# Graph attention kernel: softmax weights regrouped into four chunks of 128 rows and one of 32-row bands, row sums moved to VectorE, block-diagonal values written by DMA

## The reference

```python
def _gat_attention(self_feat, cond_adj, label_bias, Wq, bq, Wk, bk, Wout, bout):
    kv = self_feat[:, :20]                      # B, 20, 512
    qh = (self_feat @ Wq.T + bq).reshape(B, N, 16, 32)
    kh = (kv @ Wk.T + bk).reshape(B, 20, 16, 32)
    aff = einsum('bnhd,bmhd->bnhm', qh, kh) / sqrt(32)
    aff = where(cond_adj[:, :, None, :] > 0, aff, -9e15) + label_bias[:, :, None, :]
    w = softmax(aff, axis=-1)
    out_t = einsum('bnhm,bmf->bnhf', w, kv)
    return (einsum('bnhf,hgf->bnhg', out_t, Wout) + bout.reshape(16, 32)).reshape(B, N, 512)

row_zero = v.sum(-1) == 0
vcq = concat([v, where(row_zero[..., None], 0.0, q[:, None, :])], -1)
self_feat = vcq @ W_self.T + b_self
output = self_feat
for d in range(2):                              # d = 0: adj, d = 1: its transpose, first 20 targets
    output = output + _gat_attention(self_feat, A[d].sum(-1), A[d] @ w_bias + b_bias, Wq[d], ...)
return v + relu(output)
```

## Time and profile before

| | |
|---|---|
| runs | 735.38, 736.54, 736.55 us; median 736.54 |
| profiled execution | span 733.6 us from the first to the last instruction; its own time is not listed apart from the three |
| instructions | 11543 |
| busy | PE 676.3, DVE 625.7, POOL 519.8, ACT 413.0 us |
| mean granted clock of TensorE | 0.984 of full speed |
| moved by DMA | 70.64 MB, 96 GB/s on average |
| first scores / last batch's scores begin | 85.5 / 696.0 us |

### The profile page before, as it was taken

The page is one execution under the profiler, slowest core; times in us unless marked ns, Lnnn a source line. Parts: engine busy times, 40 slices in busy tenths (PEclk is TensorE's granted clock), DMA queues, the critical chain, the costliest instruction groups (busy, mean ns, idle before and its releaser), DMA issues.

```text
span 733.6 us, 11543 instructions
## 1 busy us (share of the span) xinstructions
PE 676.3 (92%) x3824; PEld 600.2 (82%) x3824; DVE 625.7 (85%) x802; ACT 413.0 (56%) x718; POOL 519.8 (71%) x436
## 2 busy tenths in 40 slices
PE   6999899998989989998989989998999989998975
PEld 6867788898878978798888978798788978798774
DVE  4656699989998889989998899889898899889863
ACT  3536355665656464764656464764566464765523
POOL 0000398949796688949796798949796798949795
PEclk9999999999999999999999999999999999999996
DMA  9634505124241505124241506033241406032101
GB/s 339 276 119 92 159 19 137 56 77 105 75 116 30 156 31 140 50 78 108 71 115 46 151 19 172 18 99 101 77 112 60 123 18 172 18 105 86 38 31 57
DMA packets 54080, 70.64 MB, mean 96 GB/s; under 512 B 25136, under 2 KB 34608, under 8 KB 53424
## 3 DMA queue, kind: packets, MB, share of 16 engines
q1 hardware_dynamic: 54064, 70.44, 32.6%
HBM read 49.68 MB, written 20.75 MB: 96 GB/s over the span
## 4 chain that ended last, share of the span: by engine, by line
PE 54%; DVE 25%; issue 10%; POOL 5%; DMA 3%; ACT 2%; POOLq 0%; SPq 0%; DVEq 0%; ACTq 0%
PE gen L369 10%; PE gen L371 10%; PE gen L370 10%; PE aff L405 7%; PE aff L424 7%; DVE xs L657 5%; DVE xl L652 4%; PE tp L434 4%; DVE xs L659 3%; PE gen L376 3%; DVE sfl L663 3%; POOL sff L922 3%; DVE z L704 2%; DVE sff L679 2%; POOL z L873 2%
## 5 line engine op out<-in xcount | busy, mean ns | idle before, releaser
L873 POOL TENSOR_TENSOR z<-cb,bx 128x320 f32<-128x320 f32 x128 | 127.0, 1013 | 46.9 <-PE tp L371 46.9
L424 PE MATMUL aff<-gh,sfh 128*128 128x320 f32 x512 | 126.1, 328 | 9.4 <-DVE sfl L663 7.0
L424 PE MATMUL aff<-gl,sfh 128*128 128x320 f32 x512 | 117.7, 311 | 0.0
L424 PE MATMUL aff<-gh,sfl 128*128 128x320 f32 x512 | 117.3, 311 | 0.0
L922 POOL TENSOR_TENSOR sff<-sff,x 128x512 f32<-128x512 f32 x64 | 83.3, 1312 | 40.8 <-ACT sff L535 40.6
L424 PEld LDWEIGHTS aff<-gh,sfh 128*128 128x128 f32 x512 | 87.6, 191 | 22.1 <-DVE sfl L663 10.4
L887 POOL TENSOR_TENSOR z<-z,mx 128x640 f32<-128x640 f32 x64 | 93.4, 1459 | 15.2 <-DVE mx L706 13.4
L369 PE MATMUL gen<-xh,w1h 128*128 128x512 f32 x256 | 101.6, 397 | 0.0
L371 PE MATMUL gen<-xh,w1l 128*128 128x512 f32 x256 | 99.9, 390 | 0.0
L370 PE MATMUL gen<-xl,w1h 128*128 128x512 f32 x256 | 99.8, 390 | 0.0
L891 POOL TENSOR_TENSOR z<-z,rcp 128x640 f32<-128x640 f32 x64 | 81.7, 1276 | 19.8 <-DVE rcp L712 19.8
(11 more groups left out here) (89 smaller groups left out, 1497.3 us busy)
## 6 DMA issues: line engine op xcount, KB each, us to landing
x<-in_x SPq DMA_DIRECT2D x64, 256.0 KB, 4.5
out_y<-sff SPq DMA_DIRECT2D x64, 256.0 KB, 2.7
msk<-in_mask SPq DMA_DIRECT2D x16, 880.0 KB, 4.8
cb<-c_scratch SPq DMA_DIRECT2D x16, 320.0 KB, 3.3
v_scratch<-x SPq DMA_DIRECT2D x16, 160.0 KB
vc<-v_scratch SPq DMA_DIRECT2D x16, 160.0 KB, 4.7
wkT<-in_wkT SPq DMA_DIRECT2D x1, 2048.0 KB, 9.8
woT<-in_woT SPq DMA_DIRECT2D x1, 2048.0 KB, 16.0
```

What stands on the lines that cost most here:

```text
L424: mm = nc.tensor.matmul(aff[:, t % 2, half, 0:SH], s, g[:, f, slot, half * SH:(half + 1) * SH], start=(f == 0 and i == 0), stop=(f == FC - ...
L873: last = nc.gpsimd.tensor_tensor(z[:, t, :].rearrange("p (g d h m) -> p g d h m", g=HG, d=D, h=H4)[:, :, d], cb[:].rearrange("p (g d h m) ...
```

## The change

The order of the 640 columns becomes (head group, head, direction, key). Of the 20 keys the first 16 of each (head, direction) make four chunks of exactly 128 rows, one for each head group; the last 4 make a fifth chunk `zr`, with 32 rows for each head group. `attend` is one group of three matmuls for each head group; `attend_rest` adds 12 matmuls over 32 rows each. Their output goes to the banks `aff` and not to `gen`, so that the next scores wait for the additions that read it.

The values are stored in two scratch tensors, and `load_v` writes them straight into the diagonal blocks of `va` and `vr`, which POOL clears once: 20 transfers where there was one, behind the outputs of the batch. POOL's `v_blocks` goes; its normalise is split in two (4 of 20 keys, then 16).

The row sums come from a second copy of x with nodes on partitions (`xn`), loaded in two halves, one batch further ahead (b + 2). DVE reduces them, a flag for each node goes to DRAM and comes back to all partitions (`store_nonzero`, `load_nonzero`). PE's `row_sums` and DVE's `x_sums` go.

b_self is left out of the self feature and added to the query bias (`query_bias`, in the prologue) and the output bias, so `sf_high` has one activation. The key products are made in eight units between the halves of `self_feat`. DVE takes 2 chunks of `xl` and 1 of `sfl` (before 3 and 2), POOL the rest. On ACT the first labels move ahead of `x_high`. In the prologue wq and xn are loaded ahead of woT.

```diff
-            def load_v(b):
-                sp.dma_start(vc[:].rearrange("p c t g -> p c (t g)"),
-                             v_dram[bass.ds(b, 1)].rearrange("o (c p) e -> p (o c) e", p=P)).then_inc(s_vin, 16)
+            def load_v(b):
+                own = va_dram[bass.ds(b, 1)].rearrange("o (h d) m (k e) -> h (o d m) k e", h=H4, e=DH)
+                rest = vr_dram[bass.ds(b, 1)].rearrange("o (h d) m (g t e) -> h g (o d m) t e", h=H4, g=HG, t=2)
+                for h in range(H4):
+                    r = h * D * MA
+                    sp.dma_start(va[r:r + D * MA, :, :, h].rearrange("p g t e -> p (g t) e").bitcast(F32), own[h]).then_inc(s_vin, 16)
+                for j in range(HG):
+                    for h in range(H4):
+                        r = (j * H4 + h) * D * MR
+                        sp.dma_start(vr[r:r + D * MR, :, h].bitcast(F32), rest[h, j]).then_inc(s_vin, 16)
...
             def batch(b, slot, i, ahead):
                 if ahead == 2 and slot == 0:
                     sp.wait_ge(s_bd, i + 1)
                     load_k(i + 1)
+                if ahead == 2:
+                    for half in range(2):
+                        sp.wait_ge(s_rsum, b * 2 + 4 + half)
+                        load_rows(b + 2, half)
                 if ahead >= 1:
                     sp.wait_ge(s_bx, b * T + T)
                     load_c(b + 1)
-                if ahead >= 2:
+                if ahead == 2:
+                    store_nonzero(b + 2)
                     sp.wait_ge(s_mk, b + 2)
                     load_mask(b + 2)
-                if ahead >= 1:
-                    sp.wait_ge(s_vb, b + 1)
-                    load_v(b + 1)
+                    sp.wait_ge(s_sfq, b * FC + 2 * FC)
+                    load_nonzero(b + 2)
                 for j in range(HG):
                     sp.wait_ge(s_y, b * HG + (j + 1))
                     sp.dma_start(out[bass.ds(b, 1), :, j].rearrange("o p n -> p (o n)"), sff[slot][:, j, :]).then_inc(s_out[slot], 16)
...
+                if ahead >= 1:
+                    sp.wait_ge(s_pv, b * HG + HG)
+                    load_v(b + 1)
```

```diff
 PE
+                if u < 2 and not first:
+                    pe.wait_ge(s_z, pair * (2 * T) - 1 + u)
+                if u >= 2:
+                    pe.wait_ge(s_gl, pair * GU + (u - 1))
...
+                    if t < 2:
+                        pe.wait_ge(s_u, b * HG + (2 * t + 2))
-                        if ahead >= 1 and t == T - 1 and f == FC // 2:
-                            row_sums(b + 1, 1 - slot)
...
+            def attend_rest(b, slot, pair):
+                pe.wait_ge(s_vin, b * (16 * VD) + 16 * VD)
+                pe.wait_ge(s_wtl, chunk(b, 1))
+                pe.wait_ge(s_z, b * T + T)
+                if slot == 1 and pair is not None:
+                    pe.wait_ge(s_gl, pair * GU + GU)
+                for k, (t, w) in enumerate(((0, wth), (0, wtl), (1, wth))):
+                    for j in range(HG):
+                        r = slice(j * H4 * D * MR, (j + 1) * H4 * D * MR)
+                        nc.tensor.matmul(pv_bank(j), vr[r, t].rearrange("p h e -> p (h e)"), w[r, 0, :], start=(k == 0), stop=False)
 DVE
-            def x_sums(n, slot):
-                dve.wait_ge(s_xh, n * FC + FC)
-                nc.vector.tensor_tensor(xs[:], x[slot][:, 0:2], x[slot][:, 2:4], ALU.add).then_inc(s_xs, 1)
-                dve.wait_ge(s_xs, n * 2 + 1)
-                nc.vector.tensor_tensor(xs[:, 0], xs[:, 0], xs[:, 1], ALU.add).then_inc(s_xs, 1)
+            def row_sums(n, half, src, s_in, count):
+                dve.wait_ge(s_in, count)
+                nc.vector.tensor_reduce(rsum[:, 2 * half:2 * half + 2], src, AX_X, ALU.add).then_inc(s_rsum, 1)
...
                 total(b, 0)
+                if ahead == 2:
+                    row_sums(b + 2, 0, xn[:], s_xnin, b * 32 + 48)
                 shift(b, 2)
-                if ahead >= 1:
-                    nonzero(n, other)
                 total(b, 1)
+                if ahead == 2:
+                    row_sums(b + 2, 1, xn[:], s_xnin, b * 32 + 64)
+                    nonzero(b + 2, True)
                 shift(b, 3)
```

More of the change, by code:

```diff
@@ L371, in parts, with self_feat @@
                 return nc.tensor.matmul(acc, ll, rh, start=False, stop=last)
-            def row_sums(n, odd):
-                pe.wait_ge(s_xs, n * 2 + 2)
-                nc.tensor.matmul(gen[:, bank(RS[odd]), :], ones[:], xs[:, 0, :], start=True, stop=True).then_inc(s_rs, 1)
-            def self_feat(n, odd, f):
+            def self_feat(n, f, between=None):
                 if f >= 2:
                     pe.wait_ge(s_sfq, n * FC + (f - 1))
-                if f == 1:
-                    pe.wait_ge(s_nz, n + 1)
-                acc = gen[:, bank(SF[odd] + f), :]
                 cols = slice(f * P, (f + 1) * P)
@@ L411, in scores, with key_products @@
-            def scores(b, slot, pair, ahead):
+                    mm = parts(gen[:, f % 2, :], (w1h[:, c, cols], w1l[:, c, cols]), (xh[:, c, :], xl[:, c, :]), c == 0, c == FC - 1)
+                    if between is not None and c % 2 == 1:
+                        if c == FC - 1:
+                            mm.then_inc(s_sf, 1)
+                        key_products(between, 2 * f + c // 2)
+                if between is None:
+                    mm.then_inc(s_sf, 1)
+            def key_products(pair, u, first=False):
+                f, k = u // G2, u % G2
+                if u == 0:
+                    pe.wait_ge(s_bd, pair + 1)
+                if u < 2 and not first:
+                    pe.wait_ge(s_z, pair * (2 * T) - 1 + u)
+                if u >= 2:
+                    pe.wait_ge(s_gl, pair * GU + (u - 1))
+                for hg in (2 * k, 2 * k + 1):
+                    for d in range(D):
+                        mm = nc.tensor.matmul(aff[:, k, hg % 2, 0:SH].rearrange("p (b h d m) -> p b h d m", b=2, h=H4, d=D)[:, :, :, d],
+                                              wq[:, hg, d, f * P:(f + 1) * P], bd[:, hg * D + d], start=True, stop=True)
+                mm.then_inc(s_g, 1)
@@ L480, in batch @@
                 if ahead >= 1:
-                    self_feat(n, odd, FC - 1)
-                if next_g:
-                    key_products(i + 1, 1)
+                    self_feat(n, FC - 1, pair)
                 transposes(b, slot, 2)
+                attend_rest(b, slot, pair)
                 transposes(b, slot, 3)
-                for j in range(HG):
-                    attend(b, slot, j, ahead)
-                    if next_g and j < 2:
-                        key_products(i + 1, j + 2)
-                    if j + 4 < SC:
-                        transposes(b, slot, j + 4)
+                attend(b, 0)
+                transposes(b, slot, 4)
+                for j in range(1, HG):
+                    attend(b, j)
             batches(pe, batch)
@@ L562, in _ @@
                                      bias=bself[:, c:c + 1]).then_inc(s_sfkh, 1)
-            for c in range(FC):
-                x_high(0, 0, 0, c)
             act.wait_ge(s_wo, 16)
@@ L799, in batch @@
                 shift(b, 0)
+                shift(b, 1)
                 if ahead >= 1:
@@ L900, in _ @@
             bias(0, 1)
-            sf_low(0, 0)
+            for f in range(FC - FL):
+                sf_low(0, 0, f)
             def batch(b, slot, i, ahead):
@@ L914, in batch @@
                 sub_max(b, 3)
-                normalise(b, 2)
-                normalise(b, 3)
-                v_blocks(b)
+                for t in range(2, T):
+                    normalise_rest(b, t)
+                    normalise(b, t)
                 if ahead >= 1:
-                    sf_low(n, 1 - slot)
+                    for f in range(FC - FL):
+                        sf_low(n, 1 - slot, f)
                 for j in range(HG):
```

542 lines of the change are left out of this document (292 added, 250 removed).

## The result

| | before | after |
|---|---|---|
| time, median | 735.99 us (735.38 to 736.55, 4 runs) | 901.16 us (899.86 to 904.66, 4 runs) |
| ratio | | 1.2249, 95% interval 1.2222 to 1.2276 |
| profiled execution, span | 733.6 us | 902.9 us (its own time 904.66) |
| mean granted clock | 0.984 | 0.893 |

A forecast was written before the change was run, and what follows sets the result against it. PE was taken as the bound (92% busy), DVE right behind. Loop start 87.5, fourteen batches 732, the last two 69.5 and 2.9 outside the span gave 892, rounded to 890 us; range 815 to 945.

The forecast's parts named there:

- The stall: 20 value-load issues on SP, 10.8 us, delay the row load; DVE's reduction waits 10 us, holding up the softmax and PE.
- T: Time in us since the scores of a batch started on PE.
- The period: Loop batches with the delayed rows: 48.7 us even and 56.9 odd, 105.6 a pair against 81.7 before.
- The other terms: Outside the seven pairs: loop start at 87.5 us, batch 0 7.5 us sooner, batches 14 and 15 34.5 and 35.
- The bands: PE's 12 attend matmuls of 32 rows each: taken at 0.9 us together, between 0.7 and 2.8.
- The clock: PE idles over 8 us in each batch and drops to its lower clock: 1.5 us a batch added.
- the rival on the other side: SP's 20 value loads issue in about 1 us, rows land when DVE asks: 723 us, 705 to 735; chance 11%.
- R + 33.3: Odd batch's length, counted from R, when the first row load lands: 55.4 us before the clock's addition.
- POOL about even, and no faster: POOL loses value blocks, gains an xl, an sfl and a split normalise: about even, no faster at the softmax's end.
- R + 24.6: Even batch's length, counted from R, when the first row load lands: 47.2 us before the clock's addition.

The follow-up runs named there:

- the experiment with one quarter: The changed kernel with all 12 band matmuls reading rows 0 to 31, instead of four quarters of the rows: 939.8 us (1.276).
- either mend: The changed kernel with the value loads moved behind the row loads on SP's queue (788.2 us), or with DVE's two row reductions moved later (789.2 us).
- four moved groups of lines: Kernel with two row buffers and the first g evicted earlier (779.4 us), plus reorderings on POOL, on DVE and ACT, and in the prologue: 739.2 us (1.004).

## Why the prediction was right, and where it was not

- **The stall.** SP's timeline, point by point: x at T = 6.7 (said 6.6), the 20 issues 10.3 us from the first to the last's end, 11.0 to the next issue (10.8), the row load at T = 18.85 (18.4), DVE's reduction at T = 23.3 (22.6). The two kinds of load are not equal, 0.76 and 0.46 apart, and only their mean fits the 0.54 I took: that the size came out so well is in part luck. The Trainium skill (DMA: Bandwidth & Descriptors, Anatomy of one DMA) gives its dispatch of some 50 ns in the account of a transfer issued from GpSimd, as one part of its fixed cost. It was no price for an issue on SP's queue, and the 0.46 and 0.76 us measured here are what such an issue takes of it.
- **The period.** Even batches of the loop behind the first took 49.2 to 49.9 us (48.7), odd ones 55.8 to 57.4 (56.9). Total 0 ended at T = 13.6, not 12, so DVE waited 9.7 and not 10; nothing hung on it.
- **The other terms.** The loop starts at 90.7, not 87.5: the key-bias products behind the last key start at 45.89 where they started at 39.65, 6.2 us later, not 3.4, and ACT waits 8.4 us for the stores of values, which I had not looked at. The 14 batches took 736.7 (732), since batch 0 gained less from its early value loads, 45.8 us (41.2). Batches 14 and 15 took 37.0 and 38.5 (34.5 and 35). Together 3.2 + 4.7 + 6.0 = 13.9, the whole difference between 889 and the span of 902.9.
- **The bands** took 0.90 us, exactly as taken. No row of before could tell 0.7 from 2.8; the reason given for the lower end, a quarter of the rows for each, is what the experiment with one quarter bears out.
- **The clock.** The lower level after the stall, as said (0.50); 1.5 us a batch taken, 0.7 to 1.1 an even batch gained when it was kept up.
- **What failed: the rival on the other side.** It said that with cheap issues the kernel would be faster, 723 us, with the sign turning near 0.1 us an issue. The runs show no such point, though none made an issue cheap: with the row load issued as early as in that case it stands at 788, without any wait for rows at 786, without rows at all at 749. Three steps of it were wrong. First, a sum: by R + 33.3 from T = 12 the odd batch is 45.3, not 43.9, which makes it 733. Second, "POOL about even, and no faster": in its total it fell, from 519.8 to 466.0 us, but the second xl and the split normalise came ahead of the maxima that the softmax waits for. Third, the DVE work was summed over the batch (39 to 35 us), and a smaller sum brought nothing forward. Even without rows, the first query addition starts at T = 23.8 in an odd batch (319.16) and 21.4 in an even one (362.79), against 21.1 (307.70) and 21.3 (352.15) before: the softmax ahead of it waits for POOL. The batches without row loads, 14 and 15, had the same optimism in them (6 us). So the direction was surer than the 0.87 I gave it, by a cause that I had not seen.
- **The stall's share.** Of the 165 us lost, either mend brings back 112 or 113; the other 52 are the orders on POOL, DVE and ACT and the reductions, of which moves of lines won back nearly all. The forecast had put 167 us on the stall (890 against its own 723) and none on the rest. The total came out because R + 24.6 and R + 33.3 count the path from the rows' landing, and those were right; what the kernel would do without the stall was wrong by 65 us.

## What to carry to other kernels

Count a transfer by its issue when it becomes twenty, and look at what stands behind it on its queue, then at what stands behind its reader. Here both had to be wrong together to cost 112 us, and either mend took it back. An engine's total says little when it is a link of a chain: ask of each moved instruction whether it stands ahead of the one that somebody waits for; four moved groups of lines were worth 40 us with the work unchanged.

## Unexpected of the hardware

- An issue on SP's queue took 0.28 us for a load of 8 partitions (2 KB) and some 0.57 for one of 32 partitions (32 KB), and the spacing was 0.46 and 0.76. For the small ones it is thus of one size with an ordinary load's 0.54.
- Three matmuls on each of four quarters of the rows took 0.92 us even when the program gives the three of a quarter in a row. The records show four starts at 445.68 and the next four at 446.01, though the program has three of one quarter ahead of the next quarter's first: a later matmul on a free quarter starts ahead of an earlier one whose quarter is busy. The Trainium skill (TensorE: Matmul & The Clock Gate, Part 3) says that matmuls start and end in program order; by that, with 0.23 us a matmul, I estimate 4 x 0.46 + 0.23 = 2.1 us for the 12 in that order, and the trace does not agree. Its 3.07x for four row tiles does agree: 2.93 / 0.92 = 3.2.
